# Rope table per pair of sequences on chip, and the large MLP weights split by GpSimd alone, in a two-layer transformer kernel

## The reference

```
layer 0: h = layernorm(x)*(1+scale)+shift     (scale, shift: cond @ W_ada.T + b_ada)
         q = h Wq (16 heads x 32); c = h Wkd; k, v = c Wku, c Wvu (4 kv heads); rope on q, k
         y = softmax(mask(q k / sqrt 32)) v;   x = x + y Wo
layer 1: h = rms(x)*w1*(1+cond @ tw1.T);  q (8 x 64), k, v (1 head); rope by pos_ids
         x = x + softmax(q k / 8) v @ Wo
         h = rms(x)*w2*(1+cond @ tw2.T);  x = x + (silu(h Wg) * (h Wu)) @ Wd    (2048 wide)
```

## Time and profile before

| | us |
|---|---|
| median of 3 runs (2061.63 to 2064.21) | 2061.93 |
| the profiled execution, whole | 2066.56 |
| its span, first to last instruction | 2064.8 |
| PE busy | 1932.5 (94%) |
| DVE busy | 1200.6 (58%) |
| ACT busy | 1052.9 (51%) |
| POOL busy | 384.8 (19%) |
| mean granted TensorE clock | 0.964 of 2.4 GHz |

### The profile page before, as it was taken

The page is one execution under the profiler, slowest core; times in us unless marked ns, Lnnn a source line. Parts: engine busy times, 40 slices in busy tenths (PEclk is TensorE's granted clock), DMA queues, the critical chain, the costliest instruction groups (busy, mean ns, idle before and its releaser), DMA issues.

```text
span 2064.8 us, 42406 instructions
## 1 busy us (share of the span) xinstructions
PE 1932.5 (94%) x14736; PEld 1162.9 (56%) x14736; DVE 1200.6 (58%) x2960; ACT 1052.9 (51%) x2957; POOL 384.8 (19%) x334
## 2 busy tenths in 40 slices
PE   6576589999999999999999999999999999999999
PEld 4463455656566655656556655656556565656544
DVE  5377755756466655756466654766456564766321
ACT  3674545735375445735375444735376444845220
POOL 8976501100111001110111001110011001110120
PEclk9567699999999999999999999999999999999999
DMA  6344011110122011210111101210111102210220
GB/s 221 98 164 166 22 42 62 63 51 12 68 73 72 16 43 62 65 50 21 68 62 56 43 33 62 72 53 21 58 63 52 51 13 76 73 62 12 72 82 21
DMA packets 58879, 127.76 MB, mean 62 GB/s; under 512 B 14608, under 2 KB 23824, under 8 KB 58640
## 3 DMA queue, kind: packets, MB, share of 16 engines
q1 hardware_dynamic: 58640, 124.71, 17.9%
HBM read 97.95 MB, written 18.35 MB: 56 GB/s over the span
## 4 chain that ended last, share of the span: by engine, by line
PE 86%; ACT 4%; DVE 4%; POOL 3%; issue 2%; DMA 0%; SPq 0%; ACTq 0%; DVEq 0%; POOLq 0%
PE gate L1251 8%; PE gate L1253 8%; PE gate L1252 8%; PE up L1251 8%; PE up L1253 8%; PE up L1252 8%; PE trans L1348 7%; PE y L1251 4%; PE y L1253 4%; PE y L1252 4%; PE score L1251 4%; PE score L1253 4%; PE score L1252 4%; PE trans L1284 2%; PE trans L1317 2%
## 5 line engine op out<-in xcount | busy, mean ns | idle before, releaser
L682 ACT ACTIVATE prob<-score,low 128x128 f32<-128x128 f32 (+2 forms) x768 | 316.0, 427 | 130.2 <-DVE low L944 81.9
L568 POOL TENSOR_TENSOR inner_t<-inner,inner_t 128x512 f16<-128x512 f32 x128 | 148.0, 1156 | 896.7 <-ACT inner_t L890 896.7
L951 DVE TENSOR_TENSOR probt_lo<-trans,probt_hi 128x512 f16<-128x512 f32 x320 | 220.6, 689 | 75.6 <-ACT probt_hi L691 74.7
L691 ACT ACTIVATE probt_hi<-trans 128x512 f16<-128x512 f32 x320 | 193.1, 603 | 108.4 <-PE trans L1348 107.2
L1348 PE MATMUL trans<-ident,prob 128*128 128x128 f32 x1280 | 204.7, 285 | 3.3 <-ACT prob L682 3.3
L1208 DVE SCALAR_TENSOR_TENSOR silu<-silu,gate 128x512 f32<-128x512 f32 x128 | 87.9, 687 | 184.9 <-ACT silu L884 184.9
L1252 PE MATMUL gate<-mlp,ring 128*128 128x512 f16 x512 | 194.5, 380 | 0.0
L1253 PE MATMUL gate<-mlp,ring 128*128 128x512 f16 x512 | 194.4, 380 | 0.0
L1251 PE MATMUL gate<-mlp,ring 128*128 128x512 f16 x512 | 194.4, 380 | 0.0
L1253 PE MATMUL up<-mlp,ring 128*128 128x512 f16 x512 | 193.9, 379 | 0.0
L1252 PE MATMUL up<-mlp,ring 128*128 128x512 f16 x512 | 193.9, 379 | 0.0
(11 more groups left out here) (162 smaller groups left out, 4402.7 us busy)
## 6 DMA issues: line engine op xcount, KB each, us to landing
ring<-wgu_dram SPq DMA_DIRECT2D x124, 512.0 KB, 3.3
x_in<-x_dram SPq DMA_DIRECT2D x18, 512.0 KB, 5.4
x_res<-x_mid SPq DMA_DIRECT2D x16, 512.0 KB, 3.4
out_dram<-x_res SPq DMA_DIRECT2D x32, 256.0 KB, 2.0
inner_t<-wg_t_dram SPq DMA_DIRECT2D x8, 512.0 KB, 3.5
inner_t<-wu_t_dram SPq DMA_DIRECT2D x8, 512.0 KB, 5.8
wgu_dram<-ring SPq DMA_DIRECT2D x8, 512.0 KB, 7.9
inner_t<-wd_t_dram SPq DMA_DIRECT2D x4, 1024.0 KB, 6.2
```

The lines of the kernel that those rows point to most:

```text
L568: pool.tensor_tensor(inner_t[:, 1, f, :], inner[:], inner_t[:, 0, f, :], ALU.subtract).then_inc(inner_low, 1)
L682: ins = act.activation(slot[:, at:at + wid], bank_[:, at:at + wid], ACT.Exp, bias=low[:, j % 2, k:k + 1], scale=-1.0, accum_out=total)
L691: act.activation(prob_t[0][:, j % SLOTS, :], trans[use % 2][:], ACT.Copy).then_inc(hi_done, 1)
L951: dve.tensor_tensor(prob_t[1][:, j % SLOTS, :], trans[T_USE[name] % 2][:], prob_t[0][:, j % SLOTS, :], ALU.subtract).then_inc(t_free, 1)
```

## The change

Two things are changed. The rope table is no longer made for all sequences at the start: pos, its float copy and the frequencies get tiles of their own; `angles(n)` makes the reduced angles of one pair (4 tiles x 32 frequencies = 128 columns, cos and sin together 256), for pair 0 at the start and for pair n+1 at step unit1_6 of pair n; ACT takes the sine at step "end" (for pair 0 first of all); `tables(n)` writes the table straight into `rope1_sb` at the start of the round. Its scratch is the half of `q_t[0]` that only layer 0 uses. The DRAM table, its stores and loads go; SP loads 16 positions per partition and pair instead. And ACT no longer writes highs of the large weights: `big_split_` on POOL does high, scale and low in 512-column instructions, the first two kinds with a second operation (times 1.0). The first seven of the twelve stand in POOL's queue ahead of the rms roots at fill2.0, three at kv1.0, two at unit1_6 (ahead of the angles). In SP's queue the load of wo1 moves from behind slab1's to behind wd0's.

```
-HIGHS_AT = {"query0.1": ["slab2"], "query1.1": ["slab3"], "unit0_3": ["slab4"], ...
-LOWS_AT = {"unit0_0": BIG[1:6], "kv1.0": BIG[6:10], "unit1_6": BIG[10:]}
+SPLIT_AT = {"fill2.0": BIG[:7], "kv1.0": BIG[7:10], "unit1_6": BIG[10:]}
+ANGLES_AT, SINES_AT = "unit1_6", "end"
...
             def layers(n, m):
+                tables(n)
                 for step, _ in PLAN:
+                    if m is None:
+                        for key in SPLIT_AT.get(step, ()):
+                            big_split_(key)
                     if step in ("fill2.0", "fill4.0"):
...
+                    if step == ANGLES_AT:
+                        need_apart(pool, s_full, count(n, S_USES, S_USE["unit0", UNITS[0] - 1] + 1),
+                                   (half_made, 1))
+                        angles((n[0], n[1] + 1))
...
+            def big_split_(key):
+                k = BIG.index(key)
+                pool.wait_ge(*landed[key])
...
+                for src, hi in big_views(key, 0):
+                    pool.tensor_scalar(hi, src, WS, 1.0, ALU.mult, ALU.mult).then_inc(big_high, 1)
+                for m, (src, _) in enumerate(big_views(key, 0)):
+                    pool.wait_ge(big_high, 4 * k + m + 1)
+                    pool.tensor_scalar(src, src, WS, 1.0, ALU.mult, ALU.mult).then_inc(
+                        big_scaled, 1)
+                for m, ((src, hi), (_, lo)) in enumerate(zip(big_views(key, 0),
+                                                             big_views(key, 1))):
+                    pool.wait_ge(big_scaled, 4 * k + m + 1)
                     ins = pool.tensor_tensor(lo, src, hi, ALU.subtract)
                 ins.then_inc(big_split, 1)
...
+            def angles(n):
...
+                need_apart(pool, pos_in, count(n, 16, 16), (half_made, 1))
+                turned(1, pool.tensor_copy(posf[:], pos[:]))
...
+            def tables(n):
+                f = HD1 // 2
+                need(pool, rope_terms, count((n[0], n[1] - 1), 12, 12))
+                need_apart(pool, sines, count(n, 1, 1), (half_made, 1))
...
+            pool.wait_ge(freq_in, 16)
+            angles((None, 0))
+            for s in BOTH:
+                ln_root((None, 0), s)
+            pool.memset(prob[:], 0.0).then_inc(prob_clear, 1)
...
+            def sines_(n):
+                need(act, angle_ready, count(n, 1, 1))
+                act.activation(reduced, reduced, ACT.Sin).then_inc(sines, 1)
...
-            for half in range(2):
-                table_store(half)
-            sp.wait_ge(table_out, 32)
-            for s in BOTH:
-                load_rope((None, 0), s)
...
-                    elif step == "unit1_0" and not last:
-                        for s in BOTH:
-                            need_apart(sp, rope_sum, count(n, 12, 10 + s + 1), (cond_used, 1))
-                            load_rope((n[0], n[1] + 1), s)
+                    elif step == "unit1_0":
+                        need_apart(sp, table_made, count(n, 1, 1), (cond_used, 1))
+                        load_pos((n[0], n[1] + (not last)))
```

More of the change, by code:

```diff
@@ L136 @@
 BIG = [f"slab{q}" for q in SLABS] + [f"wd{c}" for c in range(CH)]
[L137 to L140, removed]
-LOWS_AT = {"unit0_0": BIG[1:6], "kv1.0": BIG[6:10], "unit1_6": BIG[10:]}
+SPLIT_AT = {"fill2.0": BIG[:7], "kv1.0": BIG[7:10], "unit1_6": BIG[10:]}
 CONDITION_AT = {f"unit0_{j}": (2 + j // CH, j % CH) for j in range(2 * CH)}
-GAINS_AT, SINES_AT = "unit0_10", "query1.0"
+GAINS_AT = "unit0_10"
+ANGLES_AT, SINES_AT = "unit1_6", "end"
+TURNS = 13
 def parts_at(step):
@@ L189, in build @@
           ln2_w, tw2_t, wq1_t, wk1_t, wv1_t, wo1_t, wg_t, wu_t, wd_t, mask_c, rope0_c, freq_c,
-          rope1, wgu, out):
+          wgu, out):
     with ExitStack() as ctx:
@@ L296, in build @@
                      for at in Q1_AT] for st in stack]
[L299 to L303, removed]
+        ANGLES = DT * HD1 // 2
+        spare = q_t[0][:, H1:, :].rearrange("p h t -> p (h t)").bitcast(F32)
+        angle = spare[:, 0:ANGLES]
+        turns, reduced, whole = (
+            spare[:, at * ANGLES:(at + 2) * ANGLES].rearrange("p (c a) -> p c a", c=2)
+            for at in (1, 3, 5))
         raw_in = [sem(f"raw_in{m}") for m in range(STAGES + 2)]
-        cond_in, ln_w_in, const_in, pos_in = (
-            sem("cond_in"), sem("ln_w_in"), sem("const_in"), sem("pos_in"))
+        cond_in, ln_w_in, const_in, pos_in, freq_in = (
+            sem("cond_in"), sem("ln_w_in"), sem("const_in"), sem("pos_in"), sem("freq_in"))
         raw_high, raw_split, cond_used = sem("raw_high"), sem("raw_split"), sem("cond_used")
@@ L407, in big_views @@
             if key[:2] == "wd":
-                return [(slot, flat(wd[half])[:, at * CH * D:(at + 1) * CH * D])]
+                return [(slot[:, c * D:(c + 1) * D],
+                         flat(wd[half])[:, (at * CH + c) * D:(at * CH + c + 1) * D])
+                        for c in range(CH)]
             src = slot.rearrange("p (m c f k) -> p m f c k", m=2, c=CH, f=2)
@@ L436, in chunks_out, with load_pos @@
                         done, 16)
[L438 to L443, removed]
             def load_x(n, s):
                 sp.dma_start(x_in[:, s], x_dram[sequence(n, s)]).then_inc(x_arrived[s], 16)
-            def load_rope(n, s):
-                sp.dma_start(rope1_sb[:, s], rope_tab[sequence(n, s)]).then_inc(
-                    rope_arrived[s], 16)
+            def load_pos(n):
+                i, off = n
+                sp.dma_start(pos[:], pos_dram[off if i is None else i + off]).then_inc(pos_in, 16)
             load_x((None, 0), 0)
@@ L699, in ahead @@
                         weight_highs(step)
-                        if step == SINES_AT:
-                            for half in range(2):
-                                act.wait_ge(angle_ready, half + 1)
-                                act.activation(reduced[half], reduced[half], ACT.Sin).then_inc(
-                                    sines, 1)
                         if step == "fill2.0":
                             act.wait_ge(gains_made, 4 * CH)
-                        if step == "fill4.0":
-                            act.wait_ge(table_out, 32)
+                    if step == SINES_AT:
+                        sines_((n[0], n[1] + 1))
                 def behind(step):
```

131 lines of the change are left out of this document (50 added, 81 removed).

## The result

The changed kernel takes 2010.28 us (median of 4 runs, 2008.96 to 2015.61) against 2062.86: a ratio of 0.975 [0.973, 0.977], so 2.5% faster. The forecast was 2018.3. The profiled execution is the one of 2015.61, the slowest of the four; its span is 2013.7 against 2064.8, 51.1 less, and it is read against the profiled execution of before. The two stand 3.7 and 5.3 above their kernels' medians, so what a single stretch gained is known to a few us only.

A forecast was written before the change was run, and what follows sets the result against it. PE's matmuls bound the rounds; pair 0 waits on POOL's angles, then a chain through PE, ACT and DVE. Terms -2.1 - 19.4 - 5.3 - 17.8 + 1 = -43.6 from 2061.9 gave 2018.3 us, range 2000 to 2036.

The forecast's parts named there:

- Steps 1 and 2: Start of pair 0: earlier layernorm root of the second sequence, -2.1 us; ACT's stall for the angles gone, -19.4 us.
- Step 3: Pair 0: ACT's highs of the other slabs leave the chain of waits, -5.3 us (-3.8 to -10).
- Step 4: Pair 0 behind 170 us: four DVE lines wait less beside POOL's shorter instructions, -17.8 us (-6.5 to -26.8).
- Step 5: POOL in pair 0: a slab's split takes 9.5 to 10.1 us, hidden by at least 10 us everywhere; 0.
- Step 6: SP's queue: table stores and their wait go, wo1's load moves behind wd0, positions' loads are small; 0.
- Step 7: The rounds: ACT's sine and table loads mostly fit idle time, 0.15 us per round, +1 us.
- Rival A: ACT's table switches reach PE in every round: 2038 us; chance 8%.
- Rival B: DVE and POOL alternate, DVE's saving falls to -6.5 us and POOL's last roots come 5 late: 2035; chance 12%.
- term 4: The same as Step 4: DVE beside POOL's long instructions in pair 0, -17.8 us, low end -6.5.
- Rival C: POOL bounds pair 0, its split queue delaying fill4's roots: slower, 2078 us at 1.75 per instruction; chance 2%.
- Rival D: The 19.4 us stall in pair 0 has another reason and returns in part, at most half: 2028; chance 6%.

The follow-up runs named there:

- e1: The kernel before with the rope table change alone, ACT's highs and POOL's long scalings kept: 2048.25 us, ratio 0.9928.
- e3: The changed kernel run again unaltered: 2011.68 us, ratio 0.9755.
- e10: The changed kernel with wo1's load put back behind slab1's: 2011.54 us, ratio 0.974.
- e2: The kernel before with the changed kernel's POOL splits and wo1 load, the whole rope table still made at the start: 2032.69 us, ratio 0.9857.
- e7: The changed kernel with one operation instead of two in POOL's 512-column highs and scalings: 2037.57 us, ratio 0.9871.
- e6: The changed kernel with ACT copying instead of taking the sine for every pair but the first, so no table switches in the rounds: 2010.71 us.
- e11: The changed kernel with the rounds' sine and its table load moved from the round's end to unit1_12: 2019.55 us, ratio 0.979.
- e4: The changed kernel with POOL's splits held back while DVE works on the rope of layer 0 or layer 1: 2018.72 us, in two groups.
- e8: The changed kernel with every POOL high made five times over: 2079.4 us, ratio 1.0076.
- e12: The same kernel as e5, run again for another profile: 2015.26 us.
- e9: The changed kernel with POOL scaling each slab in one one-operation 2048-column instruction instead of four short ones: 2020.95 us, ratio 0.979.
- e5: The changed kernel with POOL's splits placed where DVE has no low halves of weights to make: median 2015.29 us, profiled execution 2002.22.

## Why the prediction was right

By its own steps, against the profiled executions.

- **Steps 1 and 2** (-2.1 and -19.4, together -21.5): the gains came 1.8 earlier and the stack of the queries 21.5, and e1, with 22.4, confirms that they are the table's. That the sum held to 0.1 in the profiled execution is luck, for two things that it leaves out cancel there. In the kernel before DVE was held beside POOL's angles as well (the lows of wq 5.24 us instead of 2.49; from the first gain to v's first low 17.3 us, in the changed kernel 12.2). And in this execution of the changed kernel DVE was held at the lows of wo. Where it was not, the stack starts at 48.52 (e3) and 48.28 (e10), 26 us earlier than before.
- **Step 3** (-5.3, the highs on the chain): up to the root of fill2 the second stretch gave 6.5 where step 3 had 3.8 of its terms. With the 3.4 us of the next point the step is nearer to 9 than to 5.3, still within its range (-3.8 to -10). e2 takes the highs from ACT and shortens POOL's instructions at once, so no run has the highs alone.
- **Step 4** (-17.8) carried the most risk and was right in size. The excess of the four lines over a round (8.95 us in the changed kernel) fell from 26.8 to 17.3 - 8.95 = 8.3 us; the estimate was 9. How it came by the 9 is not confirmed, though: if each DVE instruction waited for the rest of one POOL instruction, 0.7 us each, e7 should by my estimate show an excess of 12 (18 instructions, POOL's at 1.46 and 1.12), and it shows 2.5. With step 3's remaining 1.5 the third stretch should have gained 19.3, and it gained 24.2. Part of the rest belongs to step 3, in ACT's timeline of the kernel before:

```profile
221.89 1.91 ACT L876 ACTIVATE wd_hi<-inner_t 128x2048 f16<-128x2048 f32 x1
```

The chain of waits runs through this high of wd2 and through one of wd3 at 240.38; 1.49 us of each stand in it as "issue", and step 3, which counted only the pieces with ACT's name, left them out: 3.4 us. The clock is the other part. The same 538 matmuls were busy for 3.9 us less, but PE's pieces in the chain shrank only from 25.1 to 23.1. Other executions with the same DVE busy time in this stretch agree that not all of it counts: with PE busy for 65.5 (e10), 63.7 and 58.9 (e6) the stretch is 89.2, 87.6 and 85.6.
- **Why 2018.3 was 8 too high**, then: the clock, which the sum left out as "a few us more", for about 2; the highs of wd2 and wd3 for 3.4; DVE held beside POOL's angles, for 4 where that isn't lost again at the lows of wo; and the second stretch, for 2 to 3 that aren't taken apart here. By the spans, the sum of -43.6 stands against -54.9 in e3; 3.7 of these 11.3 us are the slow profiled execution of before.
- **Step 5** (0): a slab takes 9.2 us, a little under the 9.5 to 10.1 foreseen (9.5 to 11.8 beside DVE's lines), and the idle times ahead of the roots, 16.57, 11.09 and 8.19, are the cover that it named ("by 10 us at the least" was 2 too much).
- **Step 6** (0): e10 agrees. **Step 7** (+1): the stretch behind the third mark grew by 1.1, and e6 puts the switches at 1.4 or less.

**Rival A** (2038) is refuted by e6, and e11 shows its mechanism at another place, with three loads a round. The Trainium skill, "ScalarE: Activation LUTs", What ACT_TABLE_LOAD costs, puts a switch at about 2.66 us with a drain. In this trace a load takes 1.28, with the next instruction 0.01 behind it; no drain is seen, and the worse place cost 1.2 us a round.

**Rival B** (2035): the changed kernel's excess is 8.3, under the 14.2 of strict alternation, so term 4 did not fall to its low end. But DVE and POOL don't simply share either: e4, e8 and e12 each show one DVE instruction held through many of POOL's. The Trainium skill, "SBUF — State Buffer", Who interferes with whom, says that VectorE and GpSimd hold their shared pair of ports for a whole instruction and the other engine waits for it. e9 agrees with it as to the direction, e7 does not, and the holds of 16.92, 33.83 and 13.7 us are longer than any POOL instruction there. I weighed only the wait for the rest of one instruction, and that was the gap of the prediction. It cost the changed kernel 3.7 us at the lows of wo in one of its two profiled executions, 6.16 against 2.48, and they were 2015.61 and 2011.68 us long; and it sank e4 and e5.

**Rival C** was priced too late, and its "against" was wrong. The trace of before has one-operation instructions of 512 columns, L620 and L621, at 1.51 and 1.49 us each, not 1.34; a slab of them is 16.4 us, which is over the rival's own limit of 16. It had the roots of fill4 late only over 16 us a slab, and before eaten at 19.7. e7, at 16.2, is 27 us behind the changed kernel, since POOL is late for the roots of fill2 and unit1_3 already. With two-operation instructions at 0.59 the case was far off: that the high's fp16 output would not slow them was a guess, said as one, and it held. **Rival D** falls with steps 2 and 4.

Three things stay open. Which of the two engines gives way when both are ready isn't settled: e5 and e12 had the same work 0.4 us apart and went opposite ways. What sets DVE's smaller waits isn't either: not POOL's length alone, by e7. And no version beat the changed kernel reliably: e5 reaches 2002.22, when nothing is held, and e4 2009.04, in an execution without a trace, but six of the seven executions of e5 and e12, and three of e4's five, were at 2012.7 or above. That a kernel could keep 2002 by leaving POOL idle while DVE splits wkv and wq was not tried.

## What to carry to other kernels

Cut the execution at marks that both versions have, and ask of each stretch which engine's busy time changed: here one part of the change owned the first stretch and the other the third. Then do it again with a second profile of the same kernel: the first stretch differed by 4.4 us between two of them, and one hid what the sum had left out. When you add up the chain, look at what runs during an "issue" piece. Look for an engine's form as well as its size before moving work to it: a second operation that does nothing made POOL's instruction 2.5 times shorter; without it the same move gained 27 us less (e7). And work moved "off the critical path" onto POOL can still reach it through DVE; look at the longest DVE instruction of the trace, not at the mean of its line.

## What the runs showed that I had not expected

- A DVE instruction that reads two SBUF operands can be held through a whole run of short POOL instructions: 16.92 us in e4 (0.68 is usual), 33.83 in e8 (0.42 is usual), 14.01 for a pair in e12 (1.78 in e5). It gives one kernel two times, 2002 and 2015 in e5 and e12; in the two traces the instruction came 0.4 us apart.
- Longer POOL instructions disturbed DVE less: the four lines took 11.5 us in e7, with POOL at 1.46 us an instruction, and 17.3 in the changed kernel, at 0.59.
- On POOL a `tensor_scalar` of 128x512 with one operation took 1.46 us, with two operations 0.59. The trace of before had both already (1.51 in L620, 0.70 in L618).
- Table loads of 1.28 us cost next to nothing at the right place, 1.4 us or less in seven rounds, against 8.2 at another.
